# First attention: the transposes and the copy of the normalised rows go to the top of each step

## The reference

```python
def _L0_xattn_ref(query, key_value, Wq, bq, Wk, bk, Wv, bv, Wo, bo):
    q = (query @ Wq + bq).reshape(B, Nq, H, D).transpose(0, 2, 1, 3)      # 16 heads of 16
    k = (key_value @ Wk + bk).reshape(B, Nkv, H, D).transpose(0, 2, 1, 3)
    v = (key_value @ Wv + bv).reshape(B, Nkv, H, D).transpose(0, 2, 1, 3)
    attn = jnp.clip(jnp.einsum('bhqd,bhkd->bhqk', q, k) * scale, -CLAMP, CLAMP)
    attn = jax.nn.softmax(attn, axis=-1)
    x = jnp.einsum('bhqk,bhkd->bqhd', attn, v).reshape(B, Nq, Cq)
    return x @ Wo + bo

x = x + _L0_xattn_ref(_layernorm(x), ctx_768, ...)
x = x + _L0_ffn_ref(_layernorm(x), w_gate, w_up, w_down)      # block-quantised weights
x = x + _L1_xattn_ref(_layernorm(x), ctx_768, mask, ...)
x = x + _L1_ffn_ref(_layernorm(x), W, b, Wg, bg)              # top 2 of 8 experts
```

## Time and profile before

| | us |
|---|---|
| median of 3 runs | 1136.29 |
| lowest, highest | 1134.07, 1148.21 |
| profiled execution | 1139.05 |
| its span | 1137.3 |
| first attention in it, about | 0 to 296 |

### The profile page before, as it was taken

How to read it: one execution, slowest core, us unless ns; L and a number is a source line. 1 busy time by engine, 2 the same in 40 slices (tenths; PEclk the granted TensorE clock), 3 DMA queues, 4 the chain that set the end, 5 groups by cost and what they waited for, 6 DMA issues and landing times.

```text
span 1137.3 us, 20995 instructions
## 1 busy us (share of the span) xinstructions
PE 1053.3 (93%) x6523; PEld 891.6 (78%) x6523; DVE 944.4 (83%) x2536; ACT 699.4 (61%) x1831; POOL 485.5 (43%) x543
## 2 busy tenths in 40 slices
PE   6899999998799888789699999999999889999997
PEld 5677777887588666444598999999999878777786
DVE  4598988888677599899666799999998878888885
ACT  1566767676255689677877677777777513333333
POOL 1235454443000288776001256666655533343343
PEclk9899999999899999878899999999999989999999
DMA  9000000000133488499501410111100000000000
GB/s 283 9 1 1 1 2 1 1 2 1 77 119 118 146 281 282 172 337 352 175 1 52 120 49 1 48 47 48 48 2 2 1 1 20 28 18 18 18 18 29
DMA packets 50631, 83.31 MB, mean 73 GB/s; under 512 B 4699, under 2 KB 36271, under 8 KB 50543
## 3 DMA queue, kind: packets, MB, share of 16 engines
q1 hardware_dynamic: 49167, 81.43, 21.2%
q10 hardware_dynamic: 1376, 0.79, 0.2%
HBM read 45.98 MB, written 36.23 MB: 72 GB/s over the span
## 4 chain that ended last, share of the span: by engine, by line
PE 42%; DVE 5%; ACT 2%; issue 2%; POOL 1%; DMA 1%; DVEq 0%; POOLq 0%; ACTq 0%
PE m_ps L2420 12%; PE a_ps L1307 10%; PE a_ps L1250 9%; PE f_ps L2321 4%; PE a_ps L1265 3%; PE m_ps L2448 1%; PE m_ps L2468 1%; PE a_ps L1284 1%; DMA k_raw<-vw_scratch 1%; DVE m_xl L2618 0%; ACT f_oq L2303 0%; PE m_ps L2457 0%; DVE m_ls L2581 0%; ACT f_o L2307 0%; DVE m_g L2605 0%
## 5 line engine op out<-in xcount | busy, mean ns | idle before, releaser
L1330 ACT ACTIVATE a_U<-a_ps,a_mx 128x80 f32<-128x80 f32 x512 | 125.6, 332 | 28.0 <-DVE a_mx L1449 25.2
L2525 POOL TENSOR_TENSOR m_half<-m_half 128x512 f32<-128x512 f32 x32 | 41.1, 1283 | 128.5 <-ACT m_half L2485 128.5
L1392 POOL TENSOR_TENSOR a_xrs<-a_xve,mhalf 128x1 f32<-128x1 f32 x32 | 31.1, 970 | 151.8 <-DVE a_xve L1510 151.8
L1399 POOL TENSOR_TENSOR a_U<-a_U,a_rc 128x1280 f32<-128x1280 f32 x32 | 74.7, 2335 | 34.1 <-DVE a_rc L1439 34.1
L1062 DVE TENSOR_SCALAR a_U<-a_ps 128x320 f32<-128x320 f32 x128 | 59.3, 484 | 33.3 <-PE a_ps L860 22.0
L2420 PE MATMUL m_ps<-m_wh,m_xh 128*128 128x512 f32 x256 | 86.1, 417 | 0.0
L2492 ACT ACTIVATE m_ex<-m_ls 128x8 f32<-128x8 f32 x32 | 6.7, 209 | 128.4 <-DVE m_ls L2581 128.4
L2420 PE MATMUL m_ps<-m_wh,m_xl 128*128 128x512 f32 x256 | 80.6, 396 | 0.0
L2420 PE MATMUL m_ps<-m_wl,m_xh 128*128 128x512 f32 x256 | 80.2, 394 | 0.0
L953 PEld LDWEIGHTS a_ps<-vals,a_PT 128*128 128x128 f32 x640 | 76.4, 192 | 2.0 <-issue 0.4
L1449 DVE TENSOR_REDUCE a_mx<-a_ps 128x4 f32<-128x320 f32 x128 | 60.1, 471 | 18.8 <-PE a_ps L1250 18.8
(11 more groups left out here) (268 smaller groups left out, 3357.6 us busy)
## 6 DMA issues: line engine op xcount, KB each, us to landing
up_scratch<-f_ub SPq DMA_DIRECT2D x24, 512.0 KB, 3.1
f_ul<-up_scratch SPq DMA_DIRECT2D x24, 512.0 KB, 5.7
key_scratch<-p_keys SPq DMA_DIRECT2D x8, 640.0 KB, 6.7
vw_scratch<-p_vw SPq DMA_DIRECT2D x16, 320.0 KB, 5.8
k_raw<-key_scratch SPq DMA_DIRECT2D x8, 640.0 KB, 5.4
k_raw<-vw_scratch SPq DMA_DIRECT2D x4, 1280.0 KB, 5.9
xs<-in_x SPq DMA_DIRECT2D x4, 1024.0 KB, 12.3
h_scratch<-f_hh SPq DMA_DIRECT2D x8, 512.0 KB, 2.6
```

The costliest lines, as they stand in the source:

```text
L1330: last = act.activation(U[a.p][:, h * KP:(h + 1) * KP], bank(a, g)[:, (h % 4) * KP:(h % 4 + 1) * KP], ACT.Exp, bias=mx[a.p][:, h:h + 1])
L1399: pool.tensor_tensor(heads(U[a.p]), heads(U[a.p]), rc[a.p][:].unsqueeze(2).broadcast_to([P, H, KP]), ALU.mult).then_inc(s_N, 1)
```

## The change

On TensorE the two calls that transpose the first eight blocks of probabilities move behind the transposes of the normalised rows (and behind the weight block's). On ScalarE the copy of the transposed rows moves ahead of the first two probability copies; the copy of the weight block's high part stays behind them. Waits move with their instructions, and none is added or taken away.

```diff
@@ TensorE, body(t)
-                    if t.ok():
-                        probs_T(t, 0)
-                        probs_T(t, 1)
                     if new.ok():
                         pe.wait_ge(s_xn, new.of(lambda n: n + 1))
...
                         last.then_inc(s_xT, 1)
                         if piece(t) is not None:
                             fw.transpose(pe, X, piece(t))
+                    if t.ok():
+                        probs_T(t, 0)
+                        probs_T(t, 1)
@@ ScalarE, body(t)
-                    if t.ok():
-                        if t.t0 >= 2:
-                            act.wait_ge(s_PV, t.of(lambda n: n - 1))
-                        probs(0)
-                        probs(1)
                     if new.ok():
                         act.wait_ge(s_xT, new.of(lambda n: n + 1))
...
                         act.copy(xnT[new.p][:].rearrange("p k n -> p (k n)"), X[:, 0:D]).then_inc(s_xTe, 1)
-                        if piece(t) is not None:
-                            fw.high(act, X, piece(t))
+                    if t.ok():
+                        if t.t0 >= 2:
+                            act.wait_ge(s_PV, t.of(lambda n: n - 1))
+                        probs(0)
+                        probs(1)
+                    if new.ok() and piece(t) is not None:
+                        fw.high(act, X, piece(t))
```

## The result

| | before | after |
|---|---|---|
| median, 14 runs each, us | 1139.01 | 1132.19 |
| lowest, highest | 1134.07, 1148.21 | 1127.51, 1141.23 |
| span of the profiled execution | 1137.3 | 1131.4 |
| ratio after/before, 95% interval | | 0.9943 (0.9921 to 0.9965) |

The change makes the kernel 0.6% faster, some 6.8 us by the medians. That is clear of the runs' noise and far inside 2%.

The account below looks back on a forecast made before the run. TensorE was taken to pace the first attention, VectorE close behind at 7.83 us in quantising steps. Gains of 0.9, 3.9, 1.3 and 0.1 sum to 6.2 us: 1136.3 to 1130.1, rounded to 1130, range 1125 to 1138.

Parts of the forecast that it names:

- Start to the scores of step 2: First attention's opening: earlier row copy, TensorE held 0.4 us in step 1, scores at 62.05 instead of 62.95, gain 0.9 us.
- Steps 3 to 17: First attention, 15 steps: twelve quantising at 7.83 us, three light, 116.8 instead of 120.65 us, gain 3.9.
- the three light steps: Steps between 3 and 17 whose VectorE piece is only scales: forecast to fall to TensorE's 7.5 to 7.66 us.
- Behind them to step 27 and 28: Ten steps without quantising at 7.67 us, 76.7 instead of 78.0, gain 1.3; the last step 0.1 more.
- VectorE's round of 7.83: Time between second scores in steps with a full quantising piece; claimed as VectorE's own limit, untouched by the change.
- The shortest step: First attention, 219.55 to 227.22 us: 7.67 us, taken as TensorE's own step time without waits.
- The step without a weight piece: A first-attention step lacking the weight block's two transposes on TensorE, forecast at 7.5 us.
- The rows at the top: Row transposes now open each step: waits of about 0.1 us in VectorE-limited steps, 0.4 in step 1.
- Late rows: Rival: VectorE's rows hold every step's start, slower from 0.30 us hold on, 1137.6 to 1139 us; 10%.
- Full relief: Rival: VectorE's round is no bound, all 27 steps reach 7.67 us or below, 7.9 to 8.2 off, 1128; 8%.
- The hold at the bias copy: Rival: output product waits behind ScalarE's longer row of copies, 2 to 4 us given back, 1132 to 1134; 15%.
- The seam: Rival: TensorE's clock drop from 295 to 305 us falls elsewhere, up to 3 us either way, 1127 to 1133; 10%.

Follow-up runs that it names:

- second profile of the change: The changed kernel run again unaltered: ratio to the kernel before 0.9953 (0.9924 to 0.9981), span 1137.8 us, 15.78 us from step 0 to 2.
- The doubling: Second reduction ahead of each of the twelve large quantising pieces, in the kernels after and before the change: 129.60 and 130.07 us from step 2 to 17.
- moving the piece: Kernel with only ScalarE's order changed, quantising of steps 3 to 9 put ahead of VectorE's third clip: 52.4 us for steps 2 to 9 (54.5 without).

## Why the prediction was right, point by point

The forecast was 6.2 us off, from 1136.3 to 1130, range 1125 to 1138. Measured: 1132.19, 6.8 off, since the kernel before had its median at 1139.01 over 14 runs. The 2 us between forecast and time are the base, not the gain: 1136.29 was the median of three runs, and 14 runs gave 1139.01, close to the profiled execution's 1139.05. The interval of the ratio leaves 4 to 9 us for the gain, so the terms below are checked in the trace and not by the total.

- **The terms of the sum.** Start to the scores of step 2: forecast 0.9, measured 15.34 - 14.41 = 0.93 (in the second profile of the change the low clock from 50 to 55 us hides it). Steps 3 to 17: 3.9, measured 4.15; the three light steps take 7.49 to 7.52, where I had put 7.6. Behind them to step 27 and 28: 1.3 + 0.1, measured 85.68 - 84.12 = 1.56. Sum 6.2, measured 6.64. The 27 steps from top to top take 260.53 - 52.38 = 208.15, against my 208.9.
- **VectorE's round of 7.83** stands as forecast. The doubling shows that VectorE sets those steps, and moving the piece shows by which path.
- **The shortest step** was put at 7.67 and is 7.62: even there the load of the query products had waited some 0.05 for the copy, and I had taken 7.67 as TensorE's own. The eight steps from 19 to 26 make 0.4 us. The step without a weight piece is 7.40 or 7.41, not 7.5. Against that stand two things that I had not put into the sum: step 18, 7.83 instead of 7.67, where the output product waits behind ScalarE's longer row (in step 17, too, but there VectorE's round covers it), and step 27, 7.85, where VectorE's idle 0.49 ahead of the rows delays the transposes by 0.23. That these about cancel is luck.
- **The rows at the top.** I took 0.16 for the handover and called it a tie, 7.65 against 7.67. The handover is 0.05 to 0.06, the round through the rows 3.79 + 0.06 + 3.66 = 7.51, and TensorE's own 7.62: a slack of 0.1. The waits of 0.1 that I expected in VectorE-limited steps are on the load alone: in ten steps (4 to 10, 12, 15 and 17) it starts 0.05 after the rows and 0.02 or less ahead of its matmul, which is on time, so they cost nothing at the top. The one in step 1 is there: its transposes wait until 52.38 for the rows, at scores + 3.43, where the step before the change began at scores + 2.99.
- **The rivals.** Late rows is a true mechanism and not the case here: with rows 0.55 later the changed kernel takes 1.6 us more than the kernel before from step 2 to 28. By the arithmetic the loss begins where the round through the rows exceeds the old average; no run stands between. Full relief was ruled out by the 7.83. The hold at the bias copy cost 0.2 us (step 18), not 2 to 4. The seam is real in single runs and not tied to the change.
- **Where the profiled span's 5.9 us lie:** +1.35 up to the scores of step 0, where the granted clock over the first 45 us was 0.73 and before the change 0.95, -6.64 in the stage, nothing between the scores of step 28 and the last output transposes (25.26 and 25.27), -0.6 behind.

What I had not seen is that TensorE's half of the change does nothing for the time. My own working held it: in the long steps the copy waited for ScalarE, never for the transposes.

## What to carry to other kernels

Before moving a chain ahead on two engines, ask at each link what it waits for: its input, or its place in its own engine's queue. Here the copy was late by its place in ScalarE's queue; the transposes on TensorE had been ready for about a microsecond or more (220.84 against 221.75 in the shortest step), and moving them only gave up slack. And when two engines are this close, read the second one's round from score to score first: it tells how much of the wait can be had, and a piece of its work that stands between two engines' handovers can be moved into the time in which it waits for the other.

## What the runs showed of the hardware that I had not expected

- One and the same kernel runs with the granted clock at 0.73 or 0.95 over its first 45 us, 1.00 or 0.66 from 50 to 55, 0.86 or 0.66 around the end of the stage. The two profiled spans differ by 6.4 us, as much as the whole change, and the difference lies in these places. Steps of the steady part repeat to 0.01 us.
- A weight load that had to wait starts together with its matmul (221.41 for both), while an unheld one starts 0.11 ahead. A row transpose whose load led by only 0.02 was still on time; the query products, whose load led by 0.06, lost the missing 0.05.
- A two-operand VectorE operation over 128x768 took 1.36 instead of 0.95 us with GpSimd's output bias (128x256, two operands) beside it, and 0.95 with the reciprocal root alone beside it, which then took 1.19 instead of 0.55.
- VectorE can stand idle for 0.3 us more than usual between two operations of its own, at the same place in both profiles of the change (0.49 instead of 0.14 ahead of the last rows, L1091). With the statistics moved or the quantising doubled it isn't there; the doubled kernels have one of 0.33 elsewhere. Its cause is open.
